# Graph network, two layers on one core: products of layer 2 with one operand in PSUM, a short last tile, checked block bounds

## The reference

```python
h = relu(layernorm(x))                       # layer 1, attention
z = h @ W;  el, er = z . attn_l, z . attn_r  # 8 heads of 16
a = exp(leaky_relu(el[src] + er[dst]) - max) # per edge and head
x = x + segment_sum(z[src] * a, dst) / segment_sum(a, dst) + bias
h = relu(layernorm(x))                       # layer 2, tensor products
s, v = h[:, :32] @ W_up_s, h[:, 32:].reshape(n, 32, 3) @ W_up_v
w0, w1, w2, w3 = split(silu(silu(ef @ A1 + b1) @ A2 + b2) @ A3, 4)   # radial weights, 32 each, per edge
m = [s[src] y0 w0, (v[src] . y_v) / sqrt(3) w3, s[src] y_v w1, v[src] y0 w2]   # y0, y_v: edge_attr_4
x = x + linear_out(segment_sum(m, dst) / 10)
```

## Time and profile before

| | us |
|---|---|
| median of 3 runs (lowest, highest) | 4116.3 (4115.51, 4118.74) |
| span of the profiled execution | 4113.6 |
| POOL busy | 3030.3 (74%) |
| PE busy | 2636.9 (64%) |
| DVE busy | 2476.2 (60%) |
| ACT busy | 1011.8 (25%) |
| first gather of layer 1, of layer 2, end of the last | 72.2, 2062.1, 4094.1 |

### The profile page before, as it was taken

One profiled execution on the slowest core, in us unless ns is written; L12 is line 12 of the kernel. 1 busy time (PEld: TensorE's weight loads), 2 busy tenths in 40 slices (PEclk: granted clock), 3 DMA queues, 4 the chain that ended last, 5 costly groups with the idle time before them and its releaser, 6 DMA issues.

```text
span 4113.6 us, 43177 instructions
## 1 busy us (share of the span) xinstructions
PE 2636.9 (64%) x11218; PEld 1927.0 (47%) x11219; DVE 2476.2 (60%) x6036; ACT 1011.8 (25%) x1447; POOL 3030.3 (74%) x3146
## 2 busy tenths in 40 slices
PE   3554555445555455445477888788777777787777
PEld 2444444444444444434345555555555555555554
DVE  7444444444444444444467777777777777777776
ACT  4333323333332333333221111111111111111111
POOL 2777777777777777777667777777777777777776
PEclk8666666666666666666689999999999999999999
DMA  4222222222222222222222222222222222222221
GB/s 125 60 61 61 61 61 61 60 61 60 61 61 60 61 60 61 60 61 61 49 54 57 57 57 57 57 55 57 55 59 56 59 57 59 56 58 57 56 57 47
DMA packets 139864, 246.43 MB, mean 60 GB/s; under 512 B 54124, under 2 KB 85974, under 8 KB 139734
## 3 DMA queue, kind: packets, MB, share of 16 engines
q0 software_dynamic: 100352, 218.57, 21.4%
q1 hardware_dynamic: 39352, 26.89, 2.3%
q10 hardware_dynamic: 144, 0.80, 0.1%
HBM read 236.02 MB, written 10.03 MB: 60 GB/s over the span
## 4 chain that ended last, share of the span: by engine, by line
POOL 52%; issue 22%; PE 10%; DVE 7%; DMA 7%; DVEq 1%; ACT 1%; POOLq 0%; ACTq 0%; SPq 0%
POOL rows L434 52%; PE pair L1204 5%; DMA rows<-up_tab,idx 3%; DMA rows<-z_tab,idx 3%; PE pair L1269 3%; DVE share L957 2%; DVE acc L864 1%; DVE share L1058 1%; DVE share L1054 1%; DVE share L1050 0%; PE pair L1119 0%; DVE share L948 0%; DVE share L1063 0%; PE pair L1231 0%; ACT acc L585 0%
## 5 line engine op out<-in xcount | busy, mean ns | idle before, releaser
L434 POOL DMA_INDIRECT rows<-up_tab,idx x1568 | 1542.7, 984 | 515.5 <-issue 486.6
L434 POOL DMA_INDIRECT rows<-z_tab,idx x1568 | 1486.2, 948 | 547.8 <-issue 514.6
L1204 PE MATMUL pair<-share,acc 128*128 128x136 f32 x3136 | 760.1, 435 | 884.1 <-DVE share L957 884.1
L1204 PEld LDWEIGHTS pair<-share,acc 128*128 128x128 f32 x3136 | 704.8, 327 | 1016.8 <-DVE share L957 1016.5
L1269 PE MATMUL pair<-share,acc 128*128 128x256 f32 x3136 | 819.4, 407 | 363.5 <-DVE share L1063 363.5
L1269 PEld LDWEIGHTS pair<-share,acc 128*128 128x128 f32 x3136 | 588.2, 197 | 744.6 <-DVE share L1063 646.9
L948 DVE TENSOR_TENSOR share<-rows,share 128x64 f32<-128x64 f32 x196 | 44.2, 225 | 943.2 <-DMA rows<-z_tab,idx 943.1
L1049 DVE TENSOR_TENSOR share<-rows,y_sb 128x384 f32<-128x384 f32 x392 | 218.9, 558 | 406.9 <-DMA rows<-up_tab,idx 405.5
L1231 PE MATMUL pair<-weights_sb,share 128*128 128x256 f32 x1576 | 395.5, 396 | 31.1 <-ACT acc L578 31.1
L565 ACT ACTIVATE share<-pair,front_sb 128x512 f32<-128x512 f32 x198 | 136.0, 687 | 1028.9 <-PE pair L1221 1028.9
L1231 PEld LDWEIGHTS pair<-weights_sb,share 128*128 128x128 f32 x1576 | 313.0, 201 | 85.2 <-issue 40.3
(11 more groups left out here) (165 smaller groups left out, 2370.3 us busy)
## 6 DMA issues: line engine op xcount, KB each, us to landing
rows<-z_tab,idx POOLq DMA_INDIRECT x1568, 2.5
rows<-up_tab,idx POOLq DMA_INDIRECT x1568, 2.5
ef_sb<-in_edge_f SPq DMA_DIRECT2D x50, 128.0 KB, 2.6
z_tab<-rows SPq DMA_DIRECT2D x7, 504.0 KB, 3.2
y_sb<-in_edge_y SPq DMA_DIRECT2D x50, 64.0 KB, 1.8
x_sb<-in_x SPq DMA_DIRECT2D x7, 448.0 KB, 7.0
up_tab<-acc SPq DMA_DIRECT2D x49, 64.0 KB, 1.6
out<-x_sb SPq DMA_DIRECT2D x48, 64.0 KB
```

Of the source, the lines that this page charges most:

```text
L434: pool.indirect_dma_start(out=rows[:, s, t, 0:width], out_offset=None, in_=table, in_offset=bass.IndirectOffsetOnAxis(ap=indices[:, t:t + ...
L1204: mm = t.matmul(bank[2 + h][:, 0:MW], hot[:, s, i, :], msg[:, h, i, :], start=(i == 0), stop=(i == T - 1))
```

## The change

Four things.

1. Products of layer 2. `weigh_first` writes in place: w0 and w2 are multiplied by y0 in the PSUM pair that holds the radial weights, and `t02` is gone. L1054 and L1056 read them there. The y of a group of four tiles is copied into PSUM (`y_ps`) once per group, by DVE, and L1049 and L1060 read that copy. The first half's wait for the sums of two tiles ago moves ahead of the first product. Before the copy DVE waits for its own last message.
2. The last tile. Its edges are laid out so that the 320 real ones fill three columns (`LT` = 3) of the eight. In both layers POOL issues three gathers for it, and PE sums three columns; in layer 1 the scores, exponentials and messages also take three columns, in layer 2 only the first half is formed. To that end the last group of layer 1 on DVE and PE is written out behind the loop.
3. `blocks`: one load of two values with the bounds check skipped becomes two loads, each checked.
4. The arrays are laid out on the host accordingly.

```diff
-            _, (lo, hi) = nc.values_load_multi_w_load_instructions(
-                ready[0:1, bass.ds(at, 2)], engines=(kind,), min_val=0, max_val=NB - 1,
-                skip_runtime_bounds_check_because="they are sums of flags over NB - 1 blocks")
+            lo = eng.value_load(ready[0:1, bass.ds(at, 1)], min_val=0, max_val=NB - 1)
+            hi = eng.value_load(ready[0:1, bass.ds(at + 1, 1)], min_val=0, max_val=NB - 1)
...
+        y_ps = bank[5][:, 2 * P:3 * P].rearrange("p (u t k) -> p u t k", u=U, k=4)
...
-            def gather(s, indices, table, width, done):
-                for t in range(T):
+            def gather(s, indices, table, width, done, n=T):
+                for t in range(n):
...
-                            gather(s, idx[:, e, s, :], tab, width, (s_l1["rows0"][s], s_l1["rows1"][s]))
+                            gather(s, idx[:, e, s, :], tab, width, (s_l1["rows0"][s], s_l1["rows1"][s]),
+                                   LT if isinstance(r, int) and s == U - 1 else T)
...
-                with dve.Fori(0, GI) as q:
+                def four_tiles(q, last):
...
+                        ts = slice(0, LT if last and s == U - 1 else T)
...
+                with dve.Fori(0, GI - 1) as q:
+                    four_tiles(q, False)
+                four_tiles(GI - 1, True)
...
-                    ins = v.tensor_tensor(t02[:, hf, :, :, :], w, bc(bc(y0, 2, 2), 3, MUL), ALU.mult)
+                    ins = v.tensor_tensor(w, w, bc(bc(y0, 2, 2), 3, MUL), ALU.mult)
...
-                weigh_first(0, 0, k * (NG + 1) + 1).then_inc(s_l2["first"], 1)
+                weigh_first(0, 0, k * (NG + 1) + 1)
+                v.tensor_copy(y_ps, y_sb[:, 0]).then_inc(s_l2["first"], 1)
...
-                        for hf in range(2):
-                            dve.wait_ge(s_l1["rows0" if hf == 0 else "rows1"][s], landed)
+                        short = isinstance(r, int) and s == U - 1
+                        for hf in range(1 if short else 2):
+                            half = "rows0" if hf == 0 else "rows1"
+                            dve.wait_ge(s_l1[half][s], ROWS_IN[half][s] if short else landed)
...
-                            y_v = bc(y_sb[:, e, s, ts, 1:4], 3, MUL)
+                            y_v = bc(y_ps[:, s, ts, 1:4], 3, MUL)
...
+                            if hf == 0:
+                                dve.wait_ge(s_l1["added"][(s + 2) % U], m if s == 1 else n)
                             v.tensor_tensor(vy, vecs, y_v, ALU.mult)
                             v.tensor_tensor(sw1[:, hf, :, :], scal, w[:, :, MUL:2 * MUL], ALU.mult)\
                                 .then_inc(s_l2["weighted"], 1)
-                            if hf == 0:
-                                dve.wait_ge(s_l1["added"][(s + 2) % U], m if s == 1 else n)
                             v.tensor_tensor(cell[:, :, 0:96].rearrange("p t (i u) -> p t i u", u=MUL), vecs,
-                                            bc(t02[:, hf, :, 1, :], 2, 3), ALU.mult)
-                            v.tensor_tensor(cell[:, :, 96:128], scal, t02[:, hf, :, 0, :], ALU.mult)
+                                            bc(w[:, :, 2 * MUL:3 * MUL], 2, 3), ALU.mult)
+                            v.tensor_tensor(cell[:, :, 96:128], scal, w[:, :, 0:MUL], ALU.mult)
...
                             weigh_first(0, 1 - e, made + U)
+                            dve.wait_ge(s_l1["msg1"][s], n)
+                            v.tensor_copy(y_ps, y_sb[:, 1 - e])
...
-                        for i in range(T):
+                        tiles = LT if last and s == U - 1 else T
+                        for i in range(tiles):
                             mm = t.matmul(bank[2 + h][:, 0:MW], hot[:, s, i, :], msg[:, h, i, :],
-                                          start=(i == 0), stop=(i == T - 1))
+                                          start=(i == 0), stop=(i == tiles - 1))
...
+                        short = isinstance(r, int) and s == U - 1
+                        tiles = LT if short else T
+                        if short or hf == 1:
+                            pe.wait_ge(s_l1["msg1"][s], n)
+                        else:
+                            pe.wait_ge(s_l1["msg0"][s], n_2)
+                        for j in range(hf * HT, min(hf * HT + HT, tiles)):
```

More of the change, by code:

```diff
@@ L39 @@
 GI = NG // U
+LT = -(-(EDGES - (NG - 1) * GE) // P)
 QUADS = GI + 1
@@ L52 @@
 LW = ZW + HEADS
-assert GI % 2 == 1 and QUADS <= 64 and AHEAD == 2 and U == 4
+assert 0 < LT < HT and GI % 2 == 1 and QUADS <= 64 and AHEAD == 2 and U == 4
 assert NB == BU * BI and NG == U * GI and NG * GE >= EDGES and PAD_DST >= NODES + 3 * P and WIN + HALF - 1 <= P
@@ L464, in gather_edges @@
                         for s in range(U):
-                            hold(pool, s_l1[half][s], GI * 16 * HT)
+                            hold(pool, s_l1[half][s], ROWS_IN[half][s])
                     hold(pool, s_l1["msg1"][U - 1], (done + 1) * GI)
                     for half in ("rows0", "rows1"):
-                        pool.inc_swdge_sem(s_l1[half], [GI * 16 * HT] * U, mode="sub")
+                        pool.inc_swdge_sem(s_l1[half], ROWS_IN[half], mode="sub")
             gather_edges(z_tab, ZW, 0, 3)
@@ L549, in four_tiles @@
                     for s in range(U):
+                        ts = slice(0, LT if isinstance(r, int) and s == U - 1 else T)
                         act.wait_ge(s_l1["score"][s], n)
-                        nc.scalar.activation(a_ps[s % 2], e2_sb[:, s % 2, :, :], ACT.Exp).then_inc(s_l1["exp"][s], 1)
+                        nc.scalar.activation(a_ps[s % 2][:, ts, :], e2_sb[:, s % 2, ts, :], ACT.Exp)\
+                            .then_inc(s_l1["exp"][s], 1)
                         turned_hot((s + AHEAD) % U, q * U + (s + AHEAD), *((n, n) if s < 2 else (m, m) if s == 2 else (m, m_1)))
@@ L939, in _ @@
                         h = s % 2
-                        el_e = rows[:, s, :, MW:ZW]
-                        dve.wait_ge(s_l1["rows0"][s], landed)
-                        dve.wait_ge(s_l1["rows1"][s], landed)
+                        ts = slice(0, LT if last and s == U - 1 else T)
+                        el_e = rows[:, s, ts, MW:ZW]
+                        if last and s == U - 1:
+                            dve.wait_ge(s_l1["rows0"][s], ROWS_IN["rows0"][s])
+                        else:
+                            dve.wait_ge(s_l1["rows0"][s], landed)
+                            dve.wait_ge(s_l1["rows1"][s], landed)
                         if s == 0:
@@ L957, in _ @@
                         v.scalar_tensor_tensor(
-                            out=msg[:, h, :, :].rearrange("p t (h f) -> p t h f", f=RW),
-                            in0=bc(a_ps[h], 3, RW), scalar=1.0,
-                            in1=rows[:, s, :, 0:MW].rearrange("p t (h f) -> p t h f", f=RW),
+                            out=msg[:, h, ts, :].rearrange("p t (h f) -> p t h f", f=RW),
+                            in0=bc(a_ps[h][:, ts, :], 3, RW), scalar=1.0,
+                            in1=rows[:, s, ts, 0:MW].rearrange("p t (h f) -> p t h f", f=RW),
                             op0=ALU.min, op1=ALU.mult).then_inc(s_l1["msg1"][s], 1)
@@ L1191, in _, with four_tiles @@
                 pe.wait_ge(G["ready_set"], 1)
-                with pe.Fori(0, GI) as q:
+                def four_tiles(q, last):
                     n = pe.snap(k * GI + q + 1, min_val=1, max_val=PASSES1 * GI)
@@ L1209, in _ @@
                             blocks(pe, mybir.EngineType.PE, q + 1, map_up)
+                with pe.Fori(0, GI - 1) as q:
+                    four_tiles(q, False)
+                four_tiles(GI - 1, True)
             last_blocks(pe, map_up)
@@ L1265, in sums @@
                     def sums(s, hf):
[L1267 to L1272, removed]
+                        short = isinstance(r, int) and s == U - 1
+                        tiles = LT if short else T
+                        if short or hf == 1:
+                            pe.wait_ge(s_l1["msg1"][s], n)
+                        else:
+                            pe.wait_ge(s_l1["msg0"][s], n_2)
+                        for j in range(hf * HT, min(hf * HT + HT, tiles)):
+                            mm = t.matmul(bank[6 + s % 2][:, 0:MSG], hot[:, s, j, :], msg2[:, s % 2, hf, j % HT, :],
+                                          start=(j == 0), stop=(j == tiles - 1))
+                            if j == tiles - 1:
+                                mm.then_inc(s_l1["agg"][s], 1)
                     for s in range(U):
@@ L1300, with laid @@
     more = 64 * U * GE - EDGES
+    def laid(a, fill, n):
+        a = np.asarray(a)
+        a = np.concatenate([a, np.full((n,) + a.shape[1:], fill, a.dtype)])
+        at = slice(NG * GE - GE, NG * GE)
+        a[at] = a[at].reshape((T, P) + a.shape[1:]).swapaxes(0, 1).reshape((GE,) + a.shape[1:])
+        return a
     arrays = {
```

25 lines of the change are left out of this document (14 added, 11 removed).

## The result

The changed kernel takes 4043.6 us (median of 4 runs, 4041.0 to 4047.2), the kernel before 4117.5 us beside it: ratio 0.9827, 95% interval [0.9815, 0.9838]. The forecast was 4046.0 us. The profiled execution of after is the slowest of its four (4047.2 us), with a span of 4045.0 us; stage by stage it is compared with the 4113.6 us of the earlier trace rows. The medians are 74.0 us apart, the two profiles 68.6 us.

What follows compares the result with a forecast made beforehand. POOL's gather beat was taken as the limit. Savings of 59.6 + 6.8 + 0 + 3.9 = 70.3 us from the 4113.6 us span give 4043.3, plus 2.7 for the median 4046.0 us; own range 4040 to 4054, stretched to 4062.

Steps and rivals of the forecast that it cites:

- Pace of layer 2: Layer 2, 17th to 1560th gather: at layer 1's beat plus 7.5 us of stalls, 1934.5 us in place of 1994.1.
- the operands: Layer 2's gathers: DVE products with two SBUF operands hold POOL up; moving one to PSUM removes all 61.7 us of stretch.
- three stalls: Layer 2, POOL's waits for PE's sums: 5.9 us before, 0.5 us more for each of three, 7.5 us (5.9 to 15).
- The end of layer 1: Last tile of layer 1, three gathers for eight: the last addition moves from 2045.93 to 2039.1, 6.8 us saved (5 to 8.7).
- Start of layer 2: 17th gather of layer 2: its 6.44 us wait for PE stays and covers the copy on DVE, change 0.
- End of layer 2: Last tile of layer 2: DVE sets its only half, the last product comes earlier, 3.9 us saved (2 to 6.2).
- Cost on DVE: DVE in layer 2: products keep their lengths; copy 14 us and moved wait 29 us lie under its 405.5 us row wait.
- A: Rival for layer 2: any DVE work on gathered rows lengthens gathers, they stay at 984 ns; 4105.6 us, chance 4 in 100.
- B: Rival for layer 2: gathers meet other DVE instructions at the new beat, half the stretch returns; 4077 us, 7 in 100.
- C: Rival for layer 2: products that read or write PSUM slow down and DVE becomes the bound; 4370 us, 4 in 100.
- POOL's waits for L1269 above 45 us: Sign that the forecast of POOL's stalls for PE's sums was wrong; these waits were 28.8 us in 56 before.
- Two SBUF operands: Reading of layer 2's longer gathers: POOL is held up by a DVE product whose operands both lie in SBUF; 61.7 us.

Runs made afterwards that it cites:

- `iota` in SBUF: The changed kernel with layer 2's one-hot reading `iota` from SBUF, so that it has two SBUF operands and no gathered rows: 4081.2 us, ratio 0.9903 to before.
- with the copy: The changed kernel plus one unused 512-column SBUF-to-SBUF copy per tile of layer 2 on DVE, behind the one-hot: 4076.5 us beside 4128.3 for before, one run.
- three tiles: The changed kernel with layer 2's gathers waiting for the sums of three tiles ago, not two: 4039.3 us; again 4039.1 beside the changed kernel's 4049.8.

## Why the prediction was right

The mechanism was right and the sum close: 4043.6 for 4046.0 us, −68.6 for −70.3 us in the profiles, −74.0 us in the medians. The profiles understate the gain, as that of after is its slowest execution. Step by step:

1. *Pace of layer 2, −59.6 us.* Measured −59.88. All the stretch went (944 ns), as "the operands" demands. The stops after the start came to 4.05, 3.96, 1.00 and small ones, 8.1 us beyond the beat, for 7.5. That this part agrees is partly luck: the forecast was three stalls of the kernel before, each 0.5 us longer, and only that at 2840.68 is one of them at that length (3.96 for 3.56 before); the one at 2277.79 is new, and in the run again of after the same two gathers wait 2.66 and 1.10 us and another one 3.91.
2. *The end of layer 1, −6.8 us.* Measured −7.17. L883 stands at 2039.00, forecast 2039.1, and the chain is the one that was followed: L1172, L530, L533, L1181, L883.
3. *Start of layer 2, 0.* This step failed: +2.23 us, and POOL stops 9.18 us at the 17th gather in place of 6.44. The windows before that gather, first of after and then of before, show PE's clock lower in after:

```profile
2078.00:2084.00 6.00, 5.45 (x14) 3.81 (x15) 5.94 (x17) 1.19 (x2) 0.00 (x0) 0.60 0.00 0
```

```profile
2084.00:2089.00 5.00, 3.99 (x17) 3.16 (x18) 4.97 (x13) 1.65 (x3) 0.30 (x1) 1.00 0.00 0
```

```profile
2078.55 2.07 PE L1250 MATMUL pair<-share,weights_sb 128*128 128x512 f32 x2 [1.35 <-ACT share L570]
...
2080.42 3.05 PE L1299 MATMUL pair<-share,acc 128*128 128x256 f32 x8
```

   PE was granted 0.60 in the mean here, near its lower level (0.50, 1.2 GHz), and L1250 took 2.07 us where the same instruction (L1225) took 1.12 before. The change alone does not bring it: the run again of after, and the kernels with the short tile alone, with y in SBUF, with `iota` in SBUF and with the copy, stop for 6.8 to 7.1 us, near the 6.44 of before; those with the products alone, the weights in SBUF and the checked loads alone stop for 7.9 to 9.0, and there the clock is low. In after it had fallen already in the tile's sums at 2074.65 (2.56 us for eight passes that took 2.00 before). Why it falls in some and not in others is open: ahead of these sums PE was idle for 2.32 us in after, and for 2.33 us with y in SBUF, where they took 1.99.
4. *End of layer 2, −3.9 us.* Measured −4.32. DVE sets the last half as forecast: L1067 starts 9.21 us after the 1560th gather, for 9.25. The 0.5 us added for the wait, the copy and the check did not show.
5. *Cost on DVE.* The weighing in place was taken at 0 and costs 15 ns each, 6 us in all. The y copy takes 0.29 us, for 0.28 estimated. The moved wait was taken at 0.15 us a tile and is 0.11: where L1067 waits for no row it starts 0.04 us after the end of the sum-adding, where L1049 started 0.07 us ahead of it. The second load was taken at 0.15 us and is 0.73. All of it is under DVE's wait for rows, 333.4 us left where some 300 were forecast. By the errata table of the Trainium skill ("VectorE: DVE Perf Modes", section on the TRN2 errata) a product would by estimate have become 65 ns longer; the trace disagrees: 281 for 282 and 548 for 547 ns.
6. *The rivals.* A falls with the SBUF `iota`, and already with 944 ns. B falls with 944 ns. C falls with 333.4 us of waiting, where it asked for under 100.
7. *A marker that was badly drawn.* "POOL's waits for L1269 above 45 us" was to show the stalls; the wait read 59.3 us, but 41.7 us of it are ordinary beats. What showed the stops is the longest wait and the rows of the timeline, not the total.
8. *The reading behind it.* "Two SBUF operands" was too narrow, as the copy shows, and 15 gathers of the kernel before were held longer than it gives (last section).

## What to carry to other kernels

Where one engine gathers at a steady beat, look for members of that beat that last longer and list which instruction of the other engine was running at their start: the mean (984 for 944 ns) held 61.7 us that no wait and no idle time showed. One operand in PSUM (products, one-hot) or the result in PSUM (the copy) took DVE out of POOL's way, at no cost to the products; half the operands bought only a quarter to a third of it (some 15 and 18 of 60 us), so move all that POOL can meet. Then see how far ahead the gatherer may run: with the stretch gone, one more tile of slack was worth another 10.7 us.

## What the runs showed that was not expected

- A copy from SBUF to SBUF holds a gather just as a product of two SBUF operands does (1.05 us in place of 0.94).
- The hold goes by who starts first: 0.02 us behind the one-hot the gather still goes ahead, 0.05 us behind it waits 1.06 us.
- Not every hold of the kernel before follows that. 15 of its gathers last 1.49 to 2.16 us, more than what is left of one product would make of 0.94, and lose 12 of the 62 us. This one starts 0.14 us ahead of L1049 and is held until 0.12 us before the end of L1054, past L1050 with its operand in PSUM. Why is open; with the operands moved, none is left.

```profile
2282.67 2.16 POOL L434 DMA_INDIRECT rows<-up_tab,idx  x1 [0.30 <-issue]
2282.81 0.54 DVE L1049 TENSOR_TENSOR share<-rows,y_sb 128x384 f32<-128x384 f32 x1
...
2283.47 0.54 DVE L1054 TENSOR_TENSOR share<-rows,share 128x384 f32<-128x384 f32 x1
```

- POOL's beat in layer 1 is 1248.4 to 1248.9 ns in most profiles, but 1250.1 to 1252.9 in five: the four of one chip and, on another, that of three tiles, beside which after had 1248.8. Over 3126 gathers that is up to 13 us, as much as the kernel before differs between chips (4116 to 4128 us); whether it is the cause was not tried.
- PE's clock can fall for some microseconds in the start or the tail of a layer. Where it did, the start of layer 2 was some 2 us longer (28.83 for 26.60 us), and the end of the kernel with the short tile alone 4.9 us longer than that of after (31.31 for 26.44), of which PE's last six passes are 1.4.
